# A sequence block on one core: the first loads cut into other pieces, and fewer zero products in front

## The reference, cut to what matters

```
q = u Wq^T + bq;  k = u Wk^T + bk;  v = u Wv^T + bv      (each channel over 256 positions)
k = causal_conv(k, ssm_k_kernel) + ssm_k_D * k
kv = k x v            (outer product in a head of 16 groups x 8 x 8)
y = causal_conv(kv, ssm_kernel) + D * kv
y = sum over j of q_j * y_ij;   attn = y Wo^T + bo
x = layernorm(u + attn)
h = silu(x W1^T * s1) * (x W2^T * s2);  h = gelu(h H1^T * t1);  h = gelu(h H2^T * t2)
x = layernorm(x + h W3^T * s3)
```

## Time and profile before

| what | value |
|---|---|
| median of 3 runs | 174.91 us (174.48 to 175.04) |
| profiled execution, its own time | 174.82 us |
| its span | 173.0 us |
| PE busy | 164.4 us, 95% of the span |
| PE weight loads busy | 132.8 us, 77% |
| DVE busy | 125.0 us, 72% |
| ACT busy | 99.4 us, 57% |
| POOL busy | 79.8 us, 46% |
| moved by DMA | 9.51 MB |

### The profile page before, as it was taken

How to read it: one execution, slowest core, us unless ns; L and a number is a source line. 1 busy time by engine, 2 the same in 40 slices (tenths; PEclk the granted TensorE clock), 3 DMA queues, 4 the chain that set the end, 5 groups by cost and what they waited for, 6 DMA issues and landing times.

```text
span 173.0 us, 2538 instructions
## 1 busy us (share of the span) xinstructions
PE 164.4 (95%) x790; PEld 132.8 (77%) x790; DVE 125.0 (72%) x258; ACT 99.4 (57%) x163; POOL 79.8 (46%) x88
## 2 busy tenths in 40 slices
PE   6999998999999999999999999999999999999960
PEld 2877575757988885888888888888888888899950
DVE  1349999999999997992537989672499975341651
ACT  2260699011125319646479975768999987773320
POOL 2008699999998994980201442203008610000221
PEclk9999999999999999999999999999999999999997
DMA  4999993010000000000000000000000100000021
GB/s 122 342 288 416 314 273 97 0 30 35 0 0 4 0 0 2 0 0 4 2 0 0 0 4 0 32 29 0 4 0 2 63 0 0 0 0 4 0 99 34
DMA packets 8271, 9.51 MB, mean 55 GB/s; under 512 B 896, under 2 KB 6336, under 8 KB 8256
## 3 DMA queue, kind: packets, MB, share of 16 engines
q1 hardware_dynamic: 7824, 8.86, 16.2%
q10 hardware_dynamic: 432, 0.45, 0.8%
HBM read 8.23 MB, written 1.07 MB: 54 GB/s over the span
## 4 chain that ended last, share of the span: by engine, by line
PE 72%; POOL 13%; DVE 5%; issue 5%; ACT 2%; POOLq 1%; DVEq 0%; ACTq 0%
PE psum L852 44%; PE psum L812 9%; PE psum L811 6%; POOL kv0a L426 5%; POOL xs_b L414 4%; POOL xs_a L414 3%; PE psum L888 2%; PE psum L903 2%; PE psum L828 2%; PE psum L777 1%; DVE prod_a L606 1%; DVE xs_a L606 1%; DVE tok L591 1%; PE psum L797 1%; PE psum L775 1%
## 5 line engine op out<-in xcount | busy, mean ns | idle before, releaser
L852 PE MATMUL psum<-hidden,wr 128*128 128x512 f32 (+1 forms) x312 | 67.6, 372 | 0.0
L852 PEld LDWEIGHTS psum<-hidden,wr 128*128 128x128 f32 x312 | 54.2, 189 | 9.7
L665 DVE TENSOR_TENSOR hidden<-ring,hidden 128x512 fp32r<-128x512 f32 x36 | 27.0, 764 | 23.3 <-ACT hidden L552 23.3
L532 ACT ACTIVATE ring<-psum,scales 128x512 f32<-128x512 f32 x44 | 29.8, 688 | 18.7 <-PE psum L852 18.3
L552 ACT ACTIVATE hidden<-ring 128x512 fp32r<-128x512 f32 x44 | 26.7, 630 | 2.7 <-DVE ring L659 2.2
L426 POOL TENSOR_TENSOR kv<-tok,k 128x512 f32<-128x512 f32 x16 | 16.7, 1070 | 19.1 <-PE psum L812 16.8
L625 DVE TENSOR_REDUCE y<-qy 128x64 f32<-128x512 f32 x32 | 20.7, 672 | 0.1
L616 DVE TENSOR_TENSOR qy<-psum,tok 128x512 f32<-128x512 f32 x32 | 20.8, 676 | 0.0
L432 POOL TENSOR_TENSOR hidden<-ring,hidden 128x512 fp32r<-128x512 f32 x8 | 11.9, 1487 | 18.7 <-ACT hidden L552 18.7
L392 POOL TENSOR_SCALAR rstd<-mv 128x4 f32<-128x4 f32 (+1 forms) x9 | 2.5, 276 | 36.3 <-DVE mv L698 29.9
L812 PE MATMUL psum<-kv,toep 128*128 128x256 f32 x64 | 19.0, 379 | 0.0
(11 more groups left out here) (92 smaller groups left out, 237.8 us busy)
## 6 DMA issues: line engine op xcount, KB each, us to landing
w<-in_w SPq DMA_DIRECT2D x4, 704.0 KB, 8.5
toep<-lags_out SPq DMA_DIRECT2D x8, 256.0 KB, 5.5
tok<-in_x SPq DMA_DIRECT2D x4, 256.0 KB, 2.9
xT<-in_xT SPq DMA_DIRECT2D x3, 256.0 KB, 6.1
out_x<-tok SPq DMA_DIRECT2D x3, 256.0 KB, 2.5
spec<-in_spec SPq DMA_DIRECT2D x1, 385.0 KB, 5.1
xT<-in_xT SPq DMA_DIRECT2D x2, 128.0 KB, 3.9
out_x<-tok SPq DMA_DIRECT2D x2, 128.0 KB, 2.5
```

The costliest lines, as they stand in the source:

```text
L532: nc.scalar.activation(ring_of(b), src, func, scale=scale).then_inc(act_ready, 1)
L665: v.tensor_tensor(t[:, 1, b[2], :], ring_of(b), t[:, 0, b[2], :].bitcast(F32), ALU.subtract)\
L852: ins = nc.tensor.matmul(out, wt, xt, start=(i == 0), stop=(i == len(todo) - 1))
```

## The change

The first piece of xT holds one tile (64 KB) and the second three (192 KB), where both held two. The load of wqkv becomes two: first the 128 q columns, then the 256 k and v columns. The first product of qkv 0 waits for the q columns alone. Every second product of a qkv step waits for the k and v columns, a wait ahead of the one that was there. The second group of zero products is 128 columns wide and no longer 384.

```
-XT_PIECES = ((0, 2), (2, 4), (4, 8), (8, 12), (12, 16))
+XT_PIECES = ((0, 1), (1, 4), (4, 8), (8, 12), (12, 16))
...
-        loads = ["spec", "kd", "wqkv", "bqkv", "idft", "lags", "small"]
+        loads = ["spec", "kd", "wq", "wkv", "bqkv", "idft", "lags", "small"]
...
         def _(act):
-            act.dma_start(wqkv[:], a["wqkv"]).then_inc(loaded["wqkv"], 16)
+            act.dma_start(wqkv[:, 2 * P:], a["wqkv"][:, 2 * P:]).then_inc(loaded["wq"], 16)
+            act.dma_start(wqkv[:, 0:2 * P], a["wqkv"][:, 0:2 * P]).then_inc(loaded["wkv"], 16)
...
                     if nth[s] == 1:
-                        pe.wait_ge(loaded["wqkv"], 16)
+                        pe.wait_ge(loaded["wq"], 16)
...
                     nc.tensor.matmul(out[:, 2 * P:], xT[:, t, :], wqkv[:, 2 * P:], start=True, stop=True)
+                    pe.wait_ge(loaded["wkv"], 16)
                     pe.wait_ge(back_ready, nth["xrev", piece])
...
-WARM = (512, 384)
+WARM = (512, 128)
```

## The result

Over 20 runs the changed kernel's median is 176.01 us (174.38 to 176.80), that of before beside it 174.74 us (173.74 to 175.30): a ratio of 1.0070, 95% interval 1.0055 to 1.0085. The forecast was 175.9. The fastest run of the changed kernel lies under the median of before; its times lie over 2.4 us and those of before over 1.6. (A ratio is estimated from all single times of both kernels and need not be the quotient of the two medians.) That is the first hint at what happened, and the profiled execution does not show it.

The account below looks back on a forecast made before the run. PE's front and the chain of waits behind the spectrum were taken to bound the kernel. A late clock rise added 1.0 to 174.82, giving 175.8 for the profiled execution and 175.9 for the median; range about 175.06 to 176.9 us.

Parts of the forecast that it names:

- The forecast's step: PE's front: 1.1 us idle between tile 0's products makes the clock double late, at 9.3 us; +1.0 us, 50%.
- The middle of 7.37 and 11.2: Clock rise on PE taken at 9.3 us, half way between as before (7.37) and after a full unbroken run (11.2).
- its own signs: PE's front: wrong if pace doubles by 8 us; 0.21 us halves in tiles 2 and 3 refute the late rise.
- a term that I had put at nothing: Later chain behind the spectrum: no load ends a wait there, so later landings were taken to cost 0.
- Rival 1: Spectrum's start: clock rises as before and the spectrum waits for kd alone; +0.44 us, 175.26 us; chance 30%.
- Its lower bound of +0.15: Spectrum's start if kd lands at 8.1 us as before: PE then decides, +0.15 us.
- Rival 3: PE's front moves 0.85 us earlier if ACT's table load isn't behind the DMA issues; 174.1 us; chance 5%.
- The k and v columns: Second load on ACT's queue: taken to land at 5.1 us, with bounds 4.95 and 5.75; the upper end costs 0.6.
- bqkv: Load on ACT's queue, issued at 1.62 us: lands by 6.2 with its 4.6 us, covered by tile 0's sum.
- The added wait: Ahead of all 16 second products on PE: bounds 0 and 0.1 us a tile, taken as 0.
- The factor 1: From the spectrum to the kernel's end: a shift of the spectrum goes to the end one for one.

Follow-up runs that it names:

- the second trace: The changed kernel run once more, unaltered, for its times and another trace: median 175.36 against 174.34 us before; the traced execution took 176.48 us.
- the covered kernel: The changed kernel with zero products 512, 512 and 128 wide instead of 512 and 128: 174.87 against 174.57 us before, ratio 1.0012.

## Why the prediction was right, and where its steps were not

**The forecast's step held for the median.** The idle time between tile 0's products makes the clock rise late in many executions, and that is most of the loss: the gap alone costs 0.76 to 1.10, covering it takes 0.7 to 1.0 away. The middle of 7.37 and 11.2 was a choice, so that 175.9 met 176.01 so closely is luck in part. The four traces with 0.49 us or more of idle time ahead of tile 0's last product lie on both sides of it: before 5.6, 9.8, 10.3 and 10.8. The ten traces in which PE's timeline has 0.38 us of it or none all rose by 7.4. So an execution near the late end of my bracket occurs (10.8 against 11.2), and the median stands for executions that differ by 2 us, not for a fixed delay.

**In the first profiled execution it failed by its own signs.** I had called the forecast wrong if the pace doubles by 8 and refuted by halves of 0.21 us in tiles 2 and 3; tile 2's second product at 7.02 is followed by the next at 7.45, two halves of 0.21. The spectrum's delay, 0.25, should have equalled the loss, 1.1 us of span. That this execution took 175.96 where 175.8 was forecast for it is luck: DVE's wait for x, a term that I had put at nothing, stood in for the clock. What bears the account is the second trace, with the spectrum 2.09 late, and the two kernels in which only zero products were taken away.

**The rivals.** Rival 1, that kd alone decides, holds for such an execution as the first and has the price of the loads within its bounds: 0.25 in the trace and 0.30 in the covered kernel, where it had 0.44. Its lower bound of +0.15 doesn't follow from the working, in which PE is through with tile 3 at 8.68, 0.05 late. Rival 3, faster, failed where its row said: ACT's table load waited for the issues (3.58, forecast 3.53).

By the Trainium skill, "TensorE: Matmul & The Clock Gate", Part 1, the rise isn't tied to the kernel's start and so falls differently from run to run. Two traces of one program, before 5.6 and at 10.8, agree in kind. The Trainium skill gives 0.5 us either way; these two lie 5 us apart, and the ten traces without a long gap from 4.8 to 7.4.

**Two terms were mis-sized.** The k and v columns landed at 5.6 and 5.8, not 5.1, which came from a sum over bytes; so the gap was 1.2 to 1.5 us and the second product came at 5.61 and 5.86, not 5.30. bqkv landed at 7.3, not by 6.2, where I had kept its 4.6 us from the later issue: I called it covered, and DVE is through with the sums that waited for it only 0.16 us before it can go on with kd. What the runs show in its place is the queue. In seven traces bqkv is second among ACT's loads and lands at 5.6 to 6.0; in the other seven it is third and lands at 7.0 to 8.1, whether 16 KB were put ahead of it or wqkv was only cut in two. The rule of turns between queues that I set beside kd (Trainium skill, "DMA: Bandwidth & Descriptors", Queues, rings and completion order) fits that, but no run shows the turns themselves. For kd, where I had set it, the plain shift by one issue was right (8.5, forecast 8.6). The added wait, taken as nothing, cost nothing that shows: at the fast pace tiles follow each other by 0.65 to 0.66 us in both kernels.

**The factor 1 held** for a later front up to the last normalization: spectrum +2.09 gave +2.16, +0.26 gave +0.32. With the short zero products alone +1.08 gave +1.34, since the spectrum's first products still ran at the slow pace. It doesn't hold to the end of a single execution. Nor does it for a front that is earlier (1.12 gave 0.59), since ACT's copy of the spectrum stands behind a reversal that waits for xT.

What stays open: in how many executions the clock rises late or DVE waits for x at 26 us, since only traces show that, and there is one for each kernel and two for the changed one; and whether the gap counts or the smaller amount of work ahead of tile 0, since every edit that made or covered a long gap also changed the number of zero products.

## What to carry to other kernels

Before zero products are shortened, look at what holds the second real product and not only the first: here they had to cover up to the product from which PE doesn't stop again. A load cut in two puts every load behind it on that queue one place later, however small, and delays the engine that issues; count both before the bytes. Before a front is made faster, look which step beside it waits for a load of its own: it caps the gain. Where a kernel's times scatter more after a change, one profile may be of the wrong kind: compare the starts and paces of several.

## What the runs showed of the hardware that I had not expected

- 16 KB issued ahead of a load of 192 KB on the same queue made it land 1.9 us later (5.75 to 7.64 us), and only 0.5 of that is its later issue.
- The granted clock read 1.00 from 6 to 10 us in the changed kernel's second trace, while the halves of the k-and-v products lay 0.43 us apart, the slow pace.
- The sixth DMA issue on ACT took 0.48 us in one trace of the changed kernel and 0.69 in the other; the table load came at 3.58 and at 3.80.
- From the last normalization's start to the end of the span it took 3.5 us before, 3.6 in the changed kernel's first trace and 2.95 in its second. Half a microsecond of difference between single executions comes from there, and it hid part of the 2.16 us in the second trace (span +1.6).
